# A transformer block on one core: the last product with w2, its blocks stationary and eight columns moving

## What is computed

```python
h = jax.nn.silu(xr @ w1.T)
h = jax.nn.silu(h @ w3.T)
h = h @ w2.T
out = jnp.zeros_like(xr)
for k in range(TOP_K):
    out = out.at[indices_k[:, k]].add(gates[:, k:k + 1] * h)
```

## Time and profile before

| what | value |
|---|---|
| median of three runs | 1136.23 us |
| the profiled execution's own time | 1137.7 us |
| its span, first to last instruction | 1135.8 us |
| mean granted TensorE clock (1 is 2.4 GHz) | 0.974 |
| TensorE matmul busy | 1043.5 us, 92% of the span |
| VectorE, ScalarE, GpSimd busy | 805.0, 469.9, 415.6 us |

### The profile page before, as it was taken

One profiled execution on the slowest core, in us unless ns is written; L12 is line 12 of the kernel. 1 busy time (PEld: TensorE's weight loads), 2 busy tenths in 40 slices (PEclk: granted clock), 3 DMA queues, 4 the chain that ended last, 5 costly groups with the idle time before them and its releaser, 6 DMA issues.

```text
span 1135.8 us, 17656 instructions
## 1 busy us (share of the span) xinstructions
PE 1043.5 (92%) x6502; PEld 594.8 (52%) x6502; DVE 805.0 (71%) x1915; ACT 469.9 (41%) x714; POOL 415.6 (37%) x498
## 2 busy tenths in 40 slices
PE   4672898999999999999999999999999999999998
PEld 2461454645555455645555455645555455644452
DVE  5987688975798668975798668975798668963221
ACT  4378344263335424263335424263336424262341
POOL 2493015831267014831267014831167015820000
PEclk9786889999999999999999999999999999999999
DMA  8705983153002700153002600162002600063000
GB/s 306 193 20 107 217 205 46 38 147 114 1 20 87 191 0 0 37 149 109 0 18 92 185 0 0 37 157 101 0 18 97 181 0 0 0 166 132 1 1 2
DMA packets 129377, 90.20 MB, mean 79 GB/s; under 512 B 103135, under 2 KB 112933, under 8 KB 129341
## 3 DMA queue, kind: packets, MB, share of 16 engines
q1 hardware_dynamic: 127280, 88.16, 28.1%
q10 hardware_dynamic: 2060, 1.58, 0.5%
HBM read 47.75 MB, written 16.81 MB: 57 GB/s over the span
## 4 chain that ended last, share of the span: by engine, by line
PE 55%; DVE 21%; POOL 9%; ACT 6%; issue 6%; DMA 2%; SPq 1%; POOLq 0%; ACTq 0%; DVEq 0%
PE bank L665 39%; PE bank L539 6%; DVE ub L1227 5%; POOL xbuf L415 3%; POOL mtmp L412 3%; POOL coc L376 2%; DVE ub L1247 2%; PE bank L548 2%; DVE bst L1176 2%; DVE ub L1243 2%; ACT ub L864 2%; PE bank L612 1%; ACT h_hi L905 1%; DVE x_hi L1187 1%; DVE act_t L1344 1%
## 5 line engine op out<-in xcount | busy, mean ns | idle before, releaser
L665 PE MATMUL bank<-xt_hi,w1b 128*128 128x512 f16 x1024 | 326.4, 381 | 1.8 <-DMA xt_lo<-mrow 1.2
L665 PE MATMUL bank<-w3b,h_hi 128*128 128x512 f16 x1024 | 304.5, 379 | 0.0
L665 PE MATMUL bank<-xt_lo,w1b 128*128 128x512 f16 x512 | 194.9, 381 | 0.0
L665 PE MATMUL bank<-w3b,h_lo 128*128 128x512 f16 x512 | 194.0, 379 | 0.0
L899 ACT ACTIVATE act_t<-bank,fs 128x512 f32<-128x512 f32 x128 | 86.9, 679 | 191.3 <-PE bank L665 191.3
L1349 DVE SCALAR_TENSOR_TENSOR h_lo<-act_t,h_hi 128x512 f16<-128x512 f32 x128 | 98.8, 772 | 91.7 <-ACT h_hi L905 91.7
L665 PEld LDWEIGHTS bank<-xt_hi,w1b 128*128 128x128 f16 x1024 | 100.5, 98 | 116.9 <-issue 3.7
L905 ACT ACTIVATE h_hi<-act_t 128x512 f16<-128x512 f32 x128 | 80.8, 631 | 193.8 <-DVE act_t L1344 193.8
L1344 DVE SCALAR_TENSOR_TENSOR act_t<-act_t,bank 128x512 f32<-128x512 f32 x128 | 86.6, 676 | 100.6 <-ACT act_t L899 100.3
L665 PEld LDWEIGHTS bank<-w3b,h_hi 128*128 128x128 f16 x1024 | 98.0, 98 | 76.0
L432 POOL TENSOR_TENSOR ub<-bo_b,mcur 128x512 f32<-128x512 f32 x64 | 65.4, 1051 | 189.7 <-DVE dg L1202 176.9
(11 more groups left out here) (197 smaller groups left out, 1792.8 us busy)
## 6 DMA issues: line engine op xcount, KB each, us to landing
xbuf<-in_x_dram SPq DMA_DIRECT2D x16, 1024.0 KB, 8.7
out_dram<-xbuf SPq DMA_DIRECT2D x16, 1024.0 KB, 4.4
x_lo<-in_ctx_dram SPq DMA_DIRECT2D x16, 512.0 KB, 3.4
mrow<-in_mask_dram SPq DMA_DIRECT2D x16, 512.0 KB, 4.5
w1b<-in_w_dram SPq DMA_DIRECT2D x8, 512.0 KB, 6.7
w3b<-in_w_dram SPq DMA_DIRECT2D x8, 512.0 KB, 7.8
xbuf<-in_w_dram SPq DMA_DIRECT2D x1, 4096.0 KB, 13.7
xt_hi<-x_hi SPq DMA_TRANSPOSE x32, 3.4
```

The lines of the kernel that those rows point to most:

```text
L665: mm = pe.matmul(bk[:, :], left, right, start=d == 0 and n == 0, stop=d == FT - 1 and n == 2)
```

## The change

`result` now takes a 128 x 128 block of `w2t` as the stationary operand and moves the eight columns of `acs` past it. The product comes out turned: outputs on the partitions, eight columns for each block `n` of 128 outputs. The first call fills `att[0]` with blocks 0 to 3 of `k`, the second `att[1]` with blocks 4 to 7. Each call has 32 matmuls in place of eight. VectorE copies `att[0]` to `res` (a view of `dg`, a tile of the softmax), adds `att[1]`, and the TensorE turns `res` back to rows in eight transposes into `att[2]` and `att[3]`. The two instructions at the end read those banks.

```diff
+        res = dg[:, :, :].rearrange("p c n -> p (c n)")
...
-            def result(ks):
-
-                for h in range(2):
-                    for k in ks:
-                        mm = pe.matmul(att[h][0:NE, :], acs[:, k, :], w2t[:, k, 512 * h:512 * h + 512],
-                                       start=k == 0, stop=k == FT - 1)
-                    if k == FT - 1:
-                        mm.then_inc(sm["fin_mm"], 1)
+            def result(half):
+
+                for n in range(TT):
+                    for k in range(4 * half, 4 * half + 4):
+                        mm = pe.matmul(att[half][:, NE * n:NE * n + NE], w2t[:, k, P * n:P * n + P], acs[:, k, :],
+                                       start=k % 4 == 0, stop=k % 4 == 3)
+                mm.then_inc(sm["fin_mm"], 1)
+
+            def result_rows():
+
+                pe.wait_ge(sm["fin_sum"], 1)
+                for n in range(TT):
+                    mm = pe.transpose(att[2 + n // 4][0:NE, P * (n % 4):P * (n % 4) + P], res[:, NE * n:NE * n + NE],
+                                      ident[:, :])
+                    if n % 4 == 3:
+                        mm.then_inc(sm["fin_tr"], 1)
...
-            result(range(0, FT // 2))
+            result(0)
             gated_sum(PAIRS - 1, GROUPS - 1)
             pe.wait_ge(sm["acs_set"], 2)
-            result(range(FT // 2, FT))
+            result(1)
+            result_rows()
...
+            dve.wait_ge(sm["fin_mm"], 1)
+            dve.tensor_copy(res, att[0][:, 0:TT * NE]).then_inc(sm["fin_part"], 1)
+            dve.wait_ge(sm["fin_mm"], 2)
+            dve.wait_ge(sm["fin_part"], 1)
+            dve.tensor_tensor(res, res, att[1][:, 0:TT * NE], ALU.add).then_inc(sm["fin_sum"], 1)
             dve.wait_ge(sm["row_in"], 16)
             dve.wait_ge(sm["fs_set"], 2)
             for h in range(2):
-                dve.wait_ge(sm["fin_mm"], h + 1)
+                dve.wait_ge(sm["fin_tr"], h + 1)
                 at = slice(512 * h, 512 * h + 512)
-                dve.scalar_tensor_tensor(out=out8[:, at], in0=att[h][0:NE, :], scalar=fs[0:NE, 3:4], in1=wrs[:, at],
+                dve.scalar_tensor_tensor(out=out8[:, at], in0=att[2 + h][0:NE, :], scalar=fs[0:NE, 3:4], in1=wrs[:, at],
```

More of the change, by code:

```diff
@@ L224, in build @@
             gates_hi gates_ready
-            w2_in w2_tr w2_copy acs_set fin_mm fin_ready row_in fin_out""".split()
+            w2_in w2_tr w2_copy acs_set fin_mm fin_part fin_sum fin_tr fin_ready row_in fin_out""".split()
         sm = {n: sem(n) for n in names}
```

## The result

The changed kernel takes 1148.99 us (1148.67 to 1151.24) against 1136.42 on the same chip, 1.0113 times as long with an interval of 1.0101 to 1.0126. That is 12.6 us more. The time lies in the range of the prediction, and the direction is the one it gave the larger chance, but its likeliest case, 1138.3 us at full clock, did not come. What came is the rival that it calls the second, "the clock falls", which gave 1148.6.

A forecast was written before the change was run, and what follows sets the result against it. The last product's two halves, 14.08 us together, were taken to bound the kernel's end. First half +0.17, second +0.15 and tail +1.72 made +2.0 us, so 1138.3 us, with a range of 1136.9 to 1151.0.

The forecast's parts named there:

- likeliest case: Whole change at full clock: halves +0.17 and +0.15 us, tail +1.72, together +2.0, so 1138.3 us; chance 0.48.
- the clock falls: Rival: in the last product the clock drops to half, rows take 0.213 us; +12.4 us, 1148.6 us; chance 0.43.
- the prediction's own signs: Changed profile: prediction wrong if the last product's halves differ from 7.2 us at full clock, or if the clock falls.
- The load's price: Last product: each row with a 128-column fp32 load takes 0.11 us at full clock, so a half takes 7.20 us.
- the faster rival: Last product: loads overlap at 0.026 us a row, a half takes 1.91 us; -8.5 us, 1127.7 us; chance 0.06.
- The half-clock price: Last product: a row takes 0.213 us at half clock, so the second half takes 13.8 us, +6.6 against 7.20.
- The tail: From last matmul to write: addition, signal, four transposes, two VectorE instructions; 2.48 us against 0.76, +1.72 at full clock.
- full clock with paced loads: Last product: clock stays full and loads set the pace at 0.11 us a row; 1138.3 us; chance 0.48.
- the rival's first half: First half of the last product if the clock falls: +6.6 us at once or 0 at its end; +3.3 taken.

## Why the prediction was right, and where it was not

The range took in both clocks, so the time could lie in it whichever came. By the last of the prediction's own signs, wrong "if the clock falls", the case that it named as the likeliest was wrong, and its second was right in mechanism. That the second's 1148.6 lies so near 1148.99 is partly luck: its first half could have come out 3.3 us lower or higher, and the chain grew by 13.16 us where 12.4 was forecast.

- **The load's price held.** 0.11 us per fp32 load of 128 columns, read from two rows of line 504, was found in the 25 rows at full clock of the changed kernel and over whole halves of 7.4 us with 128 columns. The product gains nothing by the turn. That loads might overlap (the faster rival) was excluded by this.
- **The half-clock price held.** 0.213 per row, from the same line, gave 13.8 us for the second half; it took 13.84. That the row at 77.70 us was at half clock, which the prediction does not show, is in the stretch below. The Trainium skill ("TensorE: Matmul & The Clock Gate", section "LDWEIGHTS (loading the stationary operand)") has one figure for a load and names no clock with it, 107 ns for 128 columns. In this case it fits the pace at full clock, 0.11 us a row, and not the pace at half, 0.213.

```profile
77.70:78.30 0.60, 0.58 (x2) 0.49 (x2) 0.56 (x2) 0.60 (x2) 0.60 (x1) 0.50 0.00 0
```

- **The tail held, in part by luck.** Forecast 2.48 us at full clock; the kernel with 128 columns takes 2.47, from the end of its last matmul at 1133.21 to the issue of the write at 1135.68. Its pieces differ and cancel: between the transposes and the first scaling pass 0.14 us (0.02 was put down), and the two scalings take 1.40 together (1.50 without the wait ahead of the first). At half clock +0.5 was forecast, and 2.96 in all was measured. From the chain and the timeline of the kernel with 128 columns:

```profile
1125.78 7.43 PE bank L723 x64
...
1133.51 0.61 PE bank L731 x4
...
1134.26 1.40 DVE L1532 SCALAR_TENSOR_TENSOR x_lo<-bank,fs,x_hi 8x512 f32<-8x512 f32 x2 [0.80 <-PE bank L731]
1135.68 0.30 SPq L344 DMA_DIRECT2D out_dram<-x_lo  x1
```

- **The step that failed is the choice between the clocks.** The prediction put "full clock with paced loads" at 0.48 and "the clock falls" at 0.43 and named the first. What weighed for it was the stretch at 132.14 to 135.55, in which 64 of 71 rows moved only 16 columns and the clock stayed. That stretch held dense matmuls as well, as the prediction said itself, and its narrow rows are over in 1.75 us, from 133.11 to 134.69 + 0.17; in the changed kernel, too, the clock was still at 1.00 that long into the narrow rows. So it should have weighed less than the plain fact that nothing in the trace showed loads alone holding the clock. The runs with 8, 32, 64 and 128 columns settle it: the loads alone do not hold it here. The first and the last of those narrow rows in the kernel before:

```profile
133.11 0.17 PE L674 MATMUL bank<-wr_t,xt_hi 128*128 128x16 f16 x1
...
134.69 0.17 PE L674 MATMUL bank<-wr_t,xt_lo 128*128 128x16 f16 x1
```

- **The size of the rival's first half.** Half of +6.6 was put down for a fall at an unknown moment, +3.3 beside +0.17; measured +4.26, since the fall came early, 2.8 us in, with 25 rows done. In the other kernels with fp32 loads it came 1.6, 2.1, 3.2 and 3.5 us into a half, so these runs give no better forecast of this term than such bounds.

Left open: why, with 64 columns, the clock held through the first half and fell in the second, and why the fall comes at different times after a half's start.

## What to carry to other kernels

Turning a product round trades moving columns for weight loads, so read the pace of the new loads first, for the data type in question, from a row in which almost nothing moves beside them. Then ask whether the new stretch still moves enough to look busy to the clock: both sides of the TensorE were busy all the time here, and it ran at half speed. Where fp32 loads set the pace, float16 parts were the way out here, and moving unused columns in time that is paid for anyway can be worth it.

## What the runs showed of the hardware that was not expected

None of this stands in the prediction; the experiments were built to look for some of it.

- Work that is thrown away made a kernel faster: 1139.08 us with 128 columns moved for each load, 1148.99 with eight.
- Narrow float16 rows do not double at half clock: 64 rows of 16 columns took 1.75 us at a clock of 1.00 and 1.88 at 0.50, while an fp32 row with a load of 128 columns went from 0.11 to 0.21 us.
- A clock that has fallen can come back in the middle of a product: in the kernel with 8 and then 128 columns it returned 5.3 us into the wide half, at about 1132.9 us.
